# A graph network on one core: the gated messages in batches of 14, their gates in PSUM

## The chip, the core and the metric

The kernel runs on one core of one Trainium2 chip. The metric is the device time in microseconds of one execution. Three runs of the kernel before took 7233.45 us in the median (7215.12 to 7235.60).

## What is computed

Four blocks of a graph network over 6250 nodes and 200000 edges (96 features; edges sorted by their target `dst`): a graph convolution network with three layers, one with two, a message layer with gates, and attention over the edges. The change is in the third block:

```python
edge_input = jnp.concatenate([x[src], edge_attr], axis=-1)
messages = _gelu(edge_input @ mW1 + mb1) @ mW2 + mb2
gates = jax.nn.sigmoid(_gelu(edge_input @ gW1 + gb1) @ gW2 + gb2)
aggregated = jax.ops.segment_sum(messages * gates, dst, num_segments=x.shape[0])
```

`edge_attr` has 32 features. `mW2` is applied after the sum over edges, so what is summed for each node is gelu(message hidden) times gate, 96 wide, and the gate itself as a 97th column.

## The kernel before

Most of the span is the same in both kernels: lists and edge counts, five convolutions as dense products with a matrix of edge counts, and at the end dense attention. Between them lies the **sum pass** (`sum_pass` on each engine), which computes the gated sums. The products x @ mW1 and x @ gW1 with their biases have been stored to DRAM as rows of 192 numbers (`table_mg`).

The 200000 edges and some padding are 128 chunks (one in each partition) of 1568 steps. A batch is U = 16 steps, that is 16 edges in each of 128 partitions; there are 98 batches, two (h = 0 and 1) in each of ITER = 49 turns of a loop. All engines walk through the same batches and wait for each other by semaphores. For one batch:

- **SP** (SyncE) loads the 16 source indices of each partition (`si[h]`) and the edge attributes (`EA[:, h]`), one batch of the same h ahead, once the rows of batch (i, h) have landed; then it waits for the batch's sums and stores them to DRAM (`run_m`). These are all one queue, in order.
- **POOL** (GpSimd) issues 16 indirect DMAs (`gather`, L671), one for each step: each fetches 128 rows of `table_mg`, one into each partition of `G[:, h, j]`. Before a batch it waits until PE has used `G[:, h]` (`hidden_ready` of the batch two earlier) and until its indices have landed.
- **PE** (TensorE) multiplies the edge attributes by a block-diagonal weight (L933) into 8 banks of PSUM (`p_h`, two steps each), and, once the gathered rows have landed, adds them by a product with the identity (L939).
- **ACT** (ScalarE) applies gelu to each bank, into `A[:, h]` in SBUF (L1175).
- **DVE** (VectorE, `gated` and `sum_pass`) multiplies the gate half of `A` by the row of gate weights `gw2` (L1606), reduces it (L1609), waits for ACT's sigmoid in `small` (L1165), multiplies the message half by the gate (L1611), copies the gate as column 97 (L1613), and then makes a running sum over the steps, 16 dependent instructions (L1631). Where the target node changes the sum starts anew (`kp` is 0 there).

After the last batch 49 more gathers fetch, for each node, the running sum at its last edge. All 8 banks of PSUM belong to the hidden values in this stage: `p_e` (4), `p_tr` (2), `p_mm` (2).

`turns` (L381) runs a body once outside and then ITER - 1 times in a hardware loop; POOL's body has 32 gathers. The same U also sizes the batches of a second way (`scatter_pass`), which is taken only for inputs that the lists can't hold; it isn't executed here.

## Time and profile before

| | |
|---|---|
| median of three runs | 7233.45 us |
| profiled execution | 7202.21 us |
| its span | 7200.2 us |
| sum pass: first to last gather of edge rows | 2652.2 to 4967.1 us |
| POOL busy over the span | 3046.4 us (42%) |
| DVE busy over the span | 4317.5 us (60%) |
| PE busy over the span | 5293.9 us (74%) |
| hardware DMA queue / software (gathers) queue | 33.0% / 9.7% of 16 engines |

The shares are averages over stages with different limits. In the profile's map of the span in 40 slices (180 us each) the sum pass fills the slices 15 to 27. Times in the rows are from the span's start. A gather's row gives POOL's time to issue it, not the landing of its data.

### The profile page before, as it was taken

How to read it: one execution, taken by the hardware profiler on the slowest of the kernel's cores; microseconds unless marked ns; L12 is line 12 of the kernel's file. 1: busy time of each engine (PE TensorE's matmuls, PEld its weight loads, DVE VectorE, ACT ScalarE, POOL GpSimd, SP SyncE). 2: the span in 40 equal slices, each digit the busy share in tenths (PEclk: the TensorE clock that was granted, in tenths of full speed). 3: DMA queues.
4: the chain of work that ended last, by engine and by line, in shares of the span. 5: the costliest groups of instructions: out<-in, count | busy, mean ns of one | idle time of the engine just before them, and what ended most of it. 6: DMA issues, size and time to landing. Idle time of an engine off the chain costs nothing.

```text
span 7200.2 us, 99230 instructions
## 1 busy us (share of the span) xinstructions
PE 5293.9 (74%) x32240; PEld 2880.2 (40%) x32240; DVE 4317.5 (60%) x10357; ACT 2375.5 (33%) x3422; POOL 3046.4 (42%) x2919
## 2 busy tenths in 40 slices
PE   2787878999899976555555555554498888888888
PEld 2344444777677763223223222322332222222223
DVE  7999999332433445444444444444567777777776
ACT  1333333000100003223223222221156666666665
POOL 1000000000000016777777777776156666666665
PEclk8999999999899987777777777776699999999998
DMA  2111112768476856666666667665011111111110
GB/s 51 64 80 71 74 78 89 228 218 268 161 249 215 267 173 102 111 112 110 113 114 114 112 115 117 113 105 86 12 42 43 43 43 45 47 43 43 43 43 23
DMA packets 493720, 752.38 MB, mean 104 GB/s; under 512 B 294904, under 2 KB 397480, under 8 KB 487240
## 3 DMA queue, kind: packets, MB, share of 16 engines
q1 hardware_dynamic: 415336, 589.29, 33.0%
q0 software_dynamic: 78176, 160.32, 9.7%
q8 instruction: 131, 2.15, 0.1%
q14 instruction: 77, 0.63, 0.0%
HBM read 585.63 MB, written 163.82 MB: 104 GB/s over the span
## 4 chain that ended last, share of the span: by engine, by line
PE 29%; DVE 28%; POOL 16%; issue 15%; ACT 4%; DMA 3%; another core or an unknown queue 2%; DVEq 1%; SPq 1%; POOLq 0%; ACTq 0%
PE p_e L903 16%; POOL GA L671 12%; DVE VA L1784 9%; PE p_e L1021 5%; POOL VA L754 4%; ACT VA L1225 4%; DVE M L1402 4%; DVE VA L1402 4%; DVE VA L1400 2%; DVE M L1400 2%; PE p_mm L1010 2%; PE p_mm L868 2%; DMA GA<-table_mg,si 1%; PE p_tr L855 1%
## 5 line engine op out<-in xcount | busy, mean ns | idle before, releaser
L671 POOL DMA_INDIRECT GA<-table_mg,si x1568 | 1723.3, 1099 | 3187.2 <-DMA si<-in_src 2598.9
L1784 DVE TENSOR_TENSOR VA<-VA,p_mm 128x1024 f32<-128x1024 f32 (+1 forms) x1274 | 1420.6, 1156 | 482.6 <-POOL VA L754 454.0
L754 POOL TENSOR_SCALAR VA<-VA 128x1024 f32<-128x1024 f32 (+1 forms) x1274 | 1245.4, 996 | 814.1 <-ACT VA L1225 814.1
L1225 ACT ACTIVATE VA<-p_e 128x1024 f32<-128x1024 f32 (+1 forms) x1274 | 1174.4, 972 | 753.1 <-PE p_e L1021 752.9
L939 PE MATMUL p_e<-GA,C 128*128 128x384 f32 x784 | 428.1, 712 | 896.2 <-DMA GA<-table_mg,si 893.6
L1606 DVE TENSOR_TENSOR M<-GA,gw 128x1536 f32<-128x1536 f32 x98 | 172.5, 1760 | 1059.6 <-ACT GA L1175 684.8
L1035 PE MATMUL p_tr<-VA,GA 128*32 128x512 f32 (+1 forms) x5096 | 662.2, 593 | 0.5 <-DVE VA L1784 0.5
L939 PEld LDWEIGHTS p_e<-GA,C 128*128 128x128 f32 x784 | 212.2, 283 | 1100.2 <-DMA GA<-table_mg,si 945.5
L1021 PE MATMUL p_e<-T,GA 32*128 32x512 f32 x3528 | 632.8, 650 | 1.1 <-ACT VA L1225 0.8
L903 PE MATMUL p_e<-GA 128*128 128x288 bf16 x4802 | 609.6, 288 | 10.8 <-DVEq L1560 10.8
L903 PE MATMUL p_e<-GA,VA 128*128 128x288 bf16 x4802 | 608.3, 287 | 10.8 <-DVEq L1560 10.8
L1631 DVE SCALAR_TENSOR_TENSOR R<-R,kp,M 128x97 f32<-128x97 f32 x1568 | 507.1, 323 | 116.8 <-issue 0.3
L1175 ACT ACTIVATE GA<-p_e 128x384 f32<-128x384 f32 x392 | 188.5, 492 | 1176.1 <-PE p_e L939 605.3
L903 PEld LDWEIGHTS p_e<-GA 128*128 128x128 bf16 x4802 | 472.0, 98 | 132.5 <-DVEq L1560 11.2
L903 PEld LDWEIGHTS p_e<-GA,VA 128*128 128x128 bf16 x4802 | 471.5, 98 | 131.7 <-DVEq L1560 11.2
L1568 DVE TENSOR_REDUCE VA<-p_e 128x288 f32 (+1 forms) x196 | 89.7, 458 | 672.5 <-PE p_e L903 672.5
L1154 ACT ACTIVATE hT<-p_tr 96x512 f32<-96x512 f32 (+1 forms) x156 | 87.7, 565 | 1182.9 <-PE p_tr L855 1137.3
L836 PE MATMUL p_e<-VA 128*128 128x392 f16 x1176 | 284.4, 354 | 140.9 <-DVE VA L1402 113.7
L1402 DVE TENSOR_SCALAR VA<-EA 128x392 f16<-128x392 f16 x1176 | 372.2, 316 | 0.0
L1402 DVE TENSOR_SCALAR M<-EA 128x392 f16<-128x392 f16 x1176 | 372.0, 316 | 0.0
L933 PE MATMUL p_e<-BD,EA 128*128 128x384 f32 x784 | 291.6, 514 | 98.7 <-ACT GA L1175 77.9
L1130 ACT ACTIVATE GA<-p_e 128x392 bf16<-128x392 f32 x400 | 198.9, 497 | 341.1 <-PE p_e L836 341.1
(177 smaller groups left out, 6568.8 us busy)
## 6 DMA issues: line engine op xcount, KB each, us to landing
GA<-adj SPq DMA_DIRECT2D x98, 800.0 KB, 4.6
VA<-adj SPq DMA_DIRECT2D x98, 800.0 KB, 4.6
run_m<-R SPq DMA_DIRECT2D x98, 776.0 KB
GA<-adj SPq DMA_DIRECT2D x98, 768.0 KB, 4.4
VA<-adj SPq DMA_DIRECT2D x98, 768.0 KB, 4.4
H<-adj SPq DMA_DIRECT2D x56, 896.0 KB, 4.9
adj<-GA SPq DMA_DIRECT2D x25, 1568.0 KB, 5.1
adj<-VA SPq DMA_DIRECT2D x24, 1568.0 KB, 5.1
```

Of the source, the lines that this page charges most:

```text
L671: pool.indirect_dma_start(out=to, out_offset=None, in_=of, in_offset=bass.IndirectOffsetOnAxis(ap=at, axis=0)).then_inc(s, 16)
L754: pool.tensor_scalar(e, e, HIGH, LOW, ALU.min, ALU.max).then_inc(clipped, 1)
L903: mm = pe.matmul(p_e[b][:, 0:PARTS * D], blk[b][:, s * P:(s + 1) * P], parts[:, s, :, :].rearrange("p k f -> p (k f)"), start=s == 0, stop ...
L933: mm = pe.matmul(p_h[k][0:CH, 0:4 * D], EA[:, h, k // 2, :], BD[:, 2 * (k % 2):2 * (k % 2) + 2, :, :].rearrange("p a b f -> p (a b f)"), s ...
L939: pe.matmul(p_h[k][0:CH, 0:4 * D].rearrange("p (a f) -> p a f", a=2), C[0:CH, C_ID:C_ID + CH], G[0:CH, h, 2 * k:2 * k + 2, 0:2 * D], start ...
L1021: mm = pe.matmul(p_e[e][:, 0:across(b)], kT[rows, d * P:(d + 1) * P], qT[b][rows, 0:across(b)], start=True, stop=True, tile_position=(e * ...
L1035: mm = pe.matmul(p_tr[b % 2][e * HW:(e + 1) * HW, 0:across(b)], Vt[:, d, e, :], slot[k % SLOTS][:, e % 2, 0:across(b)], start=d == 0, stop ...
L1225: act.activation(slot[k % SLOTS][:, :, 0:across(b)], p_four[:, 2 * e:2 * e + 2, 0:across(b)], ACT.Exp).then_inc(exps_ready, 1)
L1400: dve.tensor_scalar(hot_lo[r], iota_lo, here[b][:, 3 * PER + k:3 * PER + k + 1], None, ALU.is_equal)
L1402: hot = dve.tensor_scalar(hot_key[r], iota_key, here[b][:, k:k + 1], None, ALU.is_equal)
L1631: op = dve.scalar_tensor_tensor(out=R[:, h, j, 0:MW], in0=before, scalar=kp[:, h, j:j + 1], in1=M[:, j, 0:MW], op0=ALU.mult, op1=ALU.add)
L1784: dve.tensor_tensor(e, e, p_mm[n % 2][:, 0:across(b)].unsqueeze(1).to_broadcast([P, 2, across(b)]), ALU.mult).then_inc(weighed, 1)
```

## The change

Batches have 14 steps instead of 16: 56 turns of two batches, 112 batches, and again 1568 steps. 14 steps fill 7 banks of PSUM. The eighth bank (`p_mm[1]`) holds a copy of the row of gate weights (`gate_row`, written once by DVE at the stage's start) and the gates (`gates`, written by ACT's sigmoid). L1606 and L1611 so read one operand from SBUF (`A`) and one from PSUM. The edge attributes of a batch still take 4 groups of 4 steps, the last with two steps of padding. POOL's gathers have a loop of their own: one turn outside, then 11 passes of a body with five turns (140 gathers). The buffers `GA` and `M` keep their size.

```diff
-U = 16
+U = 14
...
-BANKS = 8
-assert U == 2 * BANKS
+BANKS = 7
+TURN = 5
+assert U == 2 * BANKS and (ITER - 1) % TURN == 0
...
-        p_h = [*p_e, *p_tr, *p_mm]
+        p_h = [*p_e, *p_tr, p_mm[0]]
+        gate_row = p_mm[1][0:CH, 0:D]
+        gates = p_mm[1][0:CH, D:D + U]
...
-                turns(pool, body)
+                body(0)
+                with pool.Fori(0, (ITER - 1) // TURN) as i:
+                    for k in range(TURN):
+                        body(i * TURN + (k + 1))
...
-            def gate(i, h):
+            def gate(i, h, to):
                 act.wait_ge(logit_ready, i * 2 + (1 + h))
-                act.activation(small[:, 1, 0:U], small[:, 0, 0:U], ACT.Sigmoid, bias=sc[0:CH, 1:2]
-                               ).then_inc(gate_ready, 1)
+                act.activation(to, small[:, 0, 0:U], ACT.Sigmoid, bias=sc[0:CH, 1:2]).then_inc(gate_ready, 1)
...
-                        gate(i, h)
+                        gate(i, h, gates)
...
-            def gated(i, h, hid):
+            def gated(i, h, hid, row, gate):
 
                 dve.tensor_tensor(M[:, :, 0:D], hid[:, :, D:2 * D],
-                                  gw2[0:CH, :].unsqueeze(1).to_broadcast([CH, U, D]), ALU.mult)
+                                  row.unsqueeze(1).to_broadcast([CH, U, D]), ALU.mult)
                 dve.drain()
                 dve.tensor_reduce(small[:, 0, 0:U], M[:, :, 0:D], AX_X, ALU.add).then_inc(logit_ready, 1)
                 dve.wait_ge(gate_ready, i * 2 + (1 + h))
-                dve.tensor_tensor(M[:, :, 0:D], hid[:, :, 0:D],
-                                  small[:, 1, 0:U].unsqueeze(2).to_broadcast([CH, U, D]), ALU.mult)
-                return dve.tensor_copy(M[:, :, D:MW], small[:, 1, 0:U].unsqueeze(2))
+                dve.tensor_tensor(M[:, :, 0:D], hid[:, :, 0:D], gate.unsqueeze(2).to_broadcast([CH, U, D]), ALU.mult)
+                return dve.tensor_copy(M[:, :, D:MW], gate.unsqueeze(2))
 
             def sum_pass():
+
+                dve.tensor_copy(gate_row, gw2[0:CH, :])
+                dve.drain()
```

On DVE, at the start of the sum pass, the program before has (`GA` holds the gelu's output, `gw` is the row of gate weights, `small` holds logits and gates):

```order
L1619 COPY kp<-keep 128x16
L1606 TENSOR_TENSOR M<-GA,gw 128x16x96 [waits gelu_done]
L1609 TENSOR_REDUCE small<-M 128x16
L1611 TENSOR_TENSOR M<-GA,small 128x16x96 [waits gate_ready]
L1613 COPY M<-small 128x16
L1631 SCALAR_TENSOR_TENSOR R<-R,kp,M 128x97 x16
```

and now, at the same place (line numbers are those of the changed kernel):

```order
L1631 COPY p_mm<-gw 128x96
L1636 COPY kp<-keep 128x14
L1621 TENSOR_TENSOR M<-GA,p_mm 128x14x96 [waits gelu_done]
L1624 TENSOR_REDUCE small<-M 128x14
L1626 TENSOR_TENSOR M<-GA,p_mm 128x14x96 [waits gate_ready]
L1627 COPY M<-p_mm 128x14
L1648 SCALAR_TENSOR_TENSOR R<-R,kp,M 128x97 x14
```

The order is the same; both products have their second operand in PSUM, and each instruction is 14 steps wide.

On POOL, the loop of the gathers before:

```order
L385 UNCONDITIONAL_BRANCH
L385 ISA
L690 REGISTER_ALU [waits hidden_ready]
L671 DMA GA<-table_mg,si0 128x192 [waits idx_landed0]
L671 DMA GA<-table_mg,si0 128x192 x15
L671 DMA GA<-table_mg,si1 128x192 [waits hidden_ready,idx_landed1]
L671 DMA GA<-table_mg,si1 128x192 x15
L385 REGISTER_ALU
L385 COMPARE_AND_BRANCH
```

and the beginning of the loop now, with the first of its five turns and the head of the second:

```order
L705 UNCONDITIONAL_BRANCH
L705 ISA
L698 ISA [waits hidden_ready]
L679 DMA GA<-table_mg,si0 128x192 [waits idx_landed0]
L679 DMA GA<-table_mg,si0 128x192 x13
L679 DMA GA<-table_mg,si1 128x192 [waits hidden_ready,idx_landed1]
L679 DMA GA<-table_mg,si1 128x192 x13
L697 ISA
L698 ISA [waits hidden_ready]
```

The same waits stand ahead of each batch, after 14 gathers instead of 16, and the branch comes after 140 gathers instead of 32.

## Rows read from the trace of the kernel before

**Rows 1.** The page's map of the span in 40 slices, busy tenths of POOL.

```profile
POOL 1000000000000016777777777776156666666665
```

**Rows 2.** Engines by stretch: busy us of PE, PEld, DVE, ACT, POOL; PE clock, DMA share, GB/s.

```profile
2722.00:4968.00 2246.00, 1218.93 (x3087) 665.13 (x3085) 1035.03 (x2037) 647.17 (x1060) 1692.93 (x1536) 0.76 0.69 113
```

**Rows 3.** Groups by line and shape, 2700 to 5000: count, busy, mean ns; idle before.

```profile
L671 POOL DMA_INDIRECT GA<-table_mg,si x1536 | 1692.9, 1102 | 582.2 <-issue 526.5 <-remote 50.6 <-DMA si<-in_src 3.3
L1631 DVE SCALAR_TENSOR_TENSOR R<-R,kp,M 128x97 f32<-128x97 f32 x1568 | 507.1, 323 | 116.8 <-issue 0.3
L1606 DVE TENSOR_TENSOR M<-GA,gw 128x1536 f32<-128x1536 f32 x98 | 172.5, 1760 | 1059.6 <-ACT GA L1175 684.8 <-issue 373.7
L1611 DVE TENSOR_TENSOR M<-GA,small 128x1536 f32<-128x1536 f32 x98 | 172.4, 1759 | 36.7 <-ACT small L1165 32.6 <-issue 4.1
L1609 DVE TENSOR_REDUCE small<-M 128x16 f32<-128x1536 f32 x98 | 171.8, 1753 | 7.3
```

**Rows 4.** Timeline of POOL and DVE, one batch: start, duration, instruction, idle before.

```profile
3510.03 1.76 DVE L1606 TENSOR_TENSOR M<-GA,gw 128x1536 f32<-128x1536 f32 x1 [9.69 <-ACT GA L1175]
3510.38 2.23 POOL L671 DMA_INDIRECT GA<-table_mg,si  x1 [0.30 <-issue]
...
3512.92 0.94 POOL L671 DMA_INDIRECT GA<-table_mg,si  x1 [0.30 <-issue]
...
3513.99 1.76 DVE L1611 TENSOR_TENSOR M<-GA,small 128x1536 f32<-128x1536 f32 x1 [0.38 <-ACT small L1165]
3514.16 2.41 POOL L671 DMA_INDIRECT GA<-table_mg,si  x1 [0.30 <-issue]
...
3515.92 6.28 DVE L1631 SCALAR_TENSOR_TENSOR R<-R,kp,M 128x97 f32<-128x97 f32 x16
...
3518.15 0.94 POOL L671 DMA_INDIRECT GA<-table_mg,si  x1 [0.30 <-issue]
```

**Rows 5.** Timeline of DVE and POOL in the attention stage.

```profile
6003.40 4.77 DVE L1784 TENSOR_TENSOR VA<-VA,p_mm 128x1024 f32<-128x1024 f32 x4 [1.39 <-POOL VA L754]
6004.67 2.05 POOL L754 TENSOR_SCALAR VA<-VA 128x1024 f32<-128x1024 f32 x2 [0.37 <-ACT VA L1225]
```

**Rows 6.** Timeline around a long pause of POOL between two batches.

```profile
3451.88 4.81 PE L939 MATMUL p_e<-GA,C 128*128 128x384 f32 x8 [8.69 <-DMA GA<-table_mg,si]
...
3469.27 0.94 POOL L671 DMA_INDIRECT GA<-table_mg,si  x1 [0.30 <-issue]
...
3472.73 0.49 ACT L1175 ACTIVATE GA<-p_tr 128x384 f32<-128x384 f32 x1 [4.40 <-remote]
...
3475.16 0.94 POOL L671 DMA_INDIRECT GA<-table_mg,si  x1 [4.94 <-remote]
```

**Rows 7.** Timeline of POOL: one of the pauses that return every 112 gathers.

```profile
3502.86 0.94 POOL L671 DMA_INDIRECT GA<-table_mg,si  x1 [2.19 <-issue]
```

**Rows 8.** Who POOL waited for, 2700 to 4990: us, times, longest.

```profile
POOL GA L671 <- issue: 526.5, 1511, 30.9
POOL GA L671 <- remote: 50.6, 14, 5.3
POOL GA L671 <- DMA si<-in_src: 3.3, 5, 2.1
```

**Rows 9.** Timeline at the stage's beginning (third batch) and end.

```profile
2722.89 1.86 POOL L671 DMA_INDIRECT GA<-table_mg,si  x1 [30.91 <-issue]
...
4966.13 0.95 POOL L671 DMA_INDIRECT GA<-table_mg,si  x1 [0.30 <-issue]
...
5004.43 0.95 POOL L671 DMA_INDIRECT VA<-run_m,ends  x1 [37.35 <-DMA run_m<-R]
```

**Rows 10.** Timeline: a store of sums, a batch's last gather, and PE's start on it.

```profile
3522.44 0.41 SPq L512 DMA_DIRECT2D run_m<-R  x1
3523.16 0.95 POOL L671 DMA_INDIRECT GA<-table_mg,si  x1 [0.31 <-issue]
...
3533.44 4.98 PE L939 MATMUL p_e<-GA,C 128*128 128x384 f32 x8 [18.81 <-DMA GA<-table_mg,si]
```

More of the change, by code:

```diff
@@ L37 @@
 EG = 4
+UG = -(-U // EG)
 PIECES = 4
-BANKS = 8
-assert U == 2 * BANKS
+BANKS = 7
+TURN = 5
+assert U == 2 * BANKS and (ITER - 1) % TURN == 0
+ROOM = 16
 MW = D + 1
@@ L145, in build @@
         KV = VA[:, 0:TILES * 2 * D].rearrange("p (t f) -> p t f", t=TILES)
-        GA = sb("GA", [P, 2 * U * (GW + 2 * D)])
+        GA = sb("GA", [P, 2 * ROOM * (GW + 2 * D)])
         G = GA[:, 0:2 * U * GW].rearrange("p (h u f) -> p h u f", h=2, u=U)
-        A = GA[:, 2 * U * GW:].rearrange("p (h u f) -> p h u f", h=2, u=U)
+        A = GA[:, 2 * U * GW:2 * U * (GW + 2 * D)].rearrange("p (h u f) -> p h u f", h=2, u=U)
         R = sb("R", [CH, 2, U, AW])
-        M = sb("M", [CH, U, AW])
-        EA = sb("EA", [P, 2, EG, CH])
+        Mr = sb("M", [CH, ROOM, AW])
+        M = Mr[:, 0:U, :]
+        EA = sb("EA", [P, 2, UG, CH])
         keep = sb("keep", [CH, STEPS])
@@ L235, in build @@
         unit = (P + KEYS) // 2
-        m_flat = M[:, :, :].rearrange("p u f -> p (u f)")
+        m_flat = Mr[:, :, :].rearrange("p u f -> p (u f)")
         units = [m_flat[:, r * unit:(r + 1) * unit] for r in range(6)] + [
@@ L270, in build @@
         p_e = [p_four[:, k, :] for k in range(4)]
-        p_h = [*p_e, *p_tr, *p_mm]
+        p_h = [*p_e, *p_tr, p_mm[0]]
+        gate_row = p_mm[1][0:CH, 0:D]
+        gates = p_mm[1][0:CH, D:D + U]
+        pairs = [(g, c) for g in range(UG) for c in (0, 1) if EG * g + 2 * c < U]
+        assert len(pairs) == BANKS
         inputs_landed = sem("inputs_landed")
@@ L495, in load_edges @@
                     else:
[L496 removed]
+                        sp.wait_ge(edge_added, i * (2 * UG) + UG * (h - 1))
                 passed(sp, sp_passed)
[L498 removed]
+                sp.dma_start(EA[:, h, :, :], edge_t[:, bass.ds(i * (2 * UG) + UG * h, UG), :]
                              ).then_inc(edge_landed[h], 16)
@@ L911, in edge_products @@
                 pe.wait_ge(edge_landed[h], i * 16 + 16)
-                for g in range(U // EG):
-                    wait(pe, edge_added, i * (2 * U // EG) + (h * U // EG + g - 1))
+                for g in range(UG):
+                    wait(pe, edge_added, i * (2 * UG) + (h * UG + g - 1))
                     for c in (0, 1):
+                        if (g, c) not in pairs:
+                            continue
                         mm = pe.matmul(p_e[2 * (g % 2) + c][0:CH, 0:4 * D], EA[:, h, g, :],
@@ L1186, in body @@
                         if n == GATE:
-                            act.wait_ge(edge_added, i * (2 * U // EG) + (h + 1) * (U // EG))
+                            act.wait_ge(edge_added, i * (2 * UG) + (h + 1) * UG)
                             act.activation(gmg[h], gmg[h], ACT.Gelu).then_inc(gelu_done, 1)
-                            gate(i, h)
+                            gate(i, h, small[:, 1, 0:U])
                         if n == ATTEND:
@@ L1195, in body @@
                         wait_scattered(act, n, i, h)
-                        for k in range(U // 4):
-                            cp = act.activation(R[:, h, 4 * k:4 * k + 4, 0:width(n)],
-                                                p_c[k][0:CH, :].rearrange("p (u f) -> p u f", u=4)[:, :, 0:width(n)],
+                        for k in range(-(-U // 4)):
+                            n_u = min(4, U - 4 * k)
+                            cp = act.activation(R[:, h, 4 * k:4 * k + n_u, 0:width(n)],
+                                                p_c[k][0:CH, :].rearrange("p (u f) -> p u f", u=4)[:, 0:n_u, 0:width(n)],
                                                 ACT.Copy)
@@ L1593, in add_edges @@
             def add_edges(i, h):
-                for g in range(U // EG):
-                    dve.wait_ge(edge_product, i * (2 * U // EG) + (h * U // EG + g + 1))
+                for g in range(UG):
+                    dve.wait_ge(edge_product, i * (2 * UG) + (h * UG + g + 1))
                     for c in (0, 1):
+                        if (g, c) not in pairs:
+                            continue
                         rows = G[0:CH, h, EG * g + 2 * c:EG * g + 2 * c + 2, 0:2 * D]
@@ L1727, in body @@
                             dve.wait_ge(gelu_done, i * 2 + (1 + h))
-                            op = gated(i, h, gmg[h])
+                            op = gated(i, h, gmg[h], gw2[0:CH, :], small[:, 1, 0:U])
                         else:
@@ L1918 @@
         "row_heads": dst.reshape(-1, ROW)[:, 0], "src_rows": src.reshape(CH, STEPS).T, "dst_rows": dst.reshape(CH, STEPS).T,
-        "edge_t": edge_attr.reshape(CH, STEPS // EG, EG, ED).transpose(2, 3, 1, 0).reshape(P, STEPS // EG, CH),
+        "edge_t": np.pad(edge_attr.reshape(CH, 2 * ITER, U, ED), ((0, 0), (0, 0), (0, UG * EG - U), (0, 0))).reshape(
+            CH, 2 * ITER * UG, EG, ED).transpose(2, 3, 1, 0).reshape(P, 2 * ITER * UG, CH),
         "consts": shape_constants(),
```

8 lines of the change are left out of this document (3 added, 5 removed).

## The prediction

> **What bounds the kernel now.** I read the map of the span first [rows 1]: POOL works in the slices 15 to 27 and again in the attention; the change touches only the first of these, the sum pass. The table by stretch [rows 2] then gives from the third batch on 2246 us, in which POOL is busy 1693, DVE 1035, ACT 647 and PE 1219, the DMA engines 69%. The groups by line [rows 3] say what POOL's other 550 us are: nearly all idle time before a gather is "issue", spread over 1511 of them [rows 8], and the timeline shows it as 0.30 us ahead of each gather [rows 4]. So POOL issues gathers back to back, and the stage lasts as long as this: 98 x 16 = 1568 gathers in both kernels. All else waits for rows, and what makes POOL faster shortens the span one to one, as far as nothing else comes late.
>
> Its time from 2722.9 to 4967.1, 2244.2 us, for 1536 gathers, splits up so:
> - undisturbed gathers: 0.95 + 0.303 us each [rows 4], 1.253 x 1536 = 1924.6;
> - longer gathers: the mean is 1.102 instead of 0.95 [rows 3], 0.152 x 1536 = 233.5;
> - pauses: idle 582.2 [rows 3], less the 30.9 ahead of the third batch [rows 9], less 0.303 x 1536 = 465.4, leaves 86.
>
> **Longer gathers.** In the timeline of a batch a gather takes 2.23 us where it begins behind L1606, 2.41 behind L1611, and 0.94 under the reduction L1609 between the two and under the running sums L1631 behind them [rows 4]. That is up to 1.28 + 1.46 = 2.7 us for each of the 96 batches, 263 us, if every product hits one, and 233.5 were found. So it is these two products, both of whose inputs are in SBUF (`A` and `gw2` or `small`), that hold POOL up. L1631 also reads two tensors from SBUF, but is over in 0.32 us.
>
> With one input in PSUM, does the hold go? The nearest row is the attention's L1784, a product of an SBUF tile by PSUM with a broadcast, 128x1024: while four of them keep DVE busy for 4.77 us, POOL's two L754 run in 2.05 us, 1.02 each [rows 5]. POOL's instruction there reads and writes SBUF itself and isn't held. I take the gain as whole: 233.5 us. Its ends are 0 and 233.5; I see no reason for less than nothing.
>
> Ahead of this stands a rule that speaks against the change: the Trainium skill ("SBUF — State Buffer", section "Who interferes with whom") says that a two-input product with both inputs in SBUF contends only with GpSimd's reads, and infers that it doesn't delay the generation of DMA descriptors. By that, gathers wouldn't be held by the products, and the sum would lose its 233.5 us. The trace disagrees, 2.41 us behind L1611; an indirect gather has indices to read. The same section says that with at most one SBUF input the product doesn't contend at all, with which the attention's row agrees.
>
> **The rest on POOL.** The second part of the sum: the third batch waits until PE has used the first, at 2722.9 [rows 9]. By then 28 gathers are out instead of 32, so 1540 are left; PE has one bank less in each product ahead of it, some 1.3 us: start 2721.6. 1540 x 1.253 = 1929.6 us. Batches of 14 cost no gather more, and as each gather has the 0.30 us ahead of it within a batch and (apart from the pauses) between batches too, the number of batches costs POOL nothing.
>
> Pauses, 86 us: a timeline of all gathers shows 28 stretches over 0.5 us in the stage. Thirteen come every 112 gathers, one gather into a batch (2.19 us the typical one [rows 7], 33 us in all). They go by the count of gathers, not by a place in the loop, so they stay: 33. The others, 53 us, stand at the beginning of a batch: eleven of 3.6 to 5.3 us, mostly "remote" [rows 8], and four of 1 to 2 us right behind such a one, for indices. The instance: PE starts on batch 32 at 3451.9, but its banks reach ACT one by one in steps of 3 to 5 us until 3473.2, and POOL, done with batch 33 at 3470.2, goes on at 3475.2, 25 us after the last gather of batch 32 [rows 6]. All eleven have these 25 us (24 to 27). Why ACT gets them so slowly the trace doesn't say. POOL's cover is one batch of gathers, undisturbed 16 x 1.253 = 20.0 us. Now it is 14 x 1.253 = 17.5: the same event costs 7.5 us instead of 5, and eleven cost 82. Behind each the indices come late more often, since SP issues them behind the wait for the batch's sums: 14 us in all, by the four such waits before. I take 96 us in place of 53. The bounds are 0 (the events go) and, if one batch in five has one, 22 x 8.7 = 191.
>
> **The loop.** Both bodies end in one branch. Of the eleven long pauses three are at the loop's turn and eight at the middle of the body, and at most of the other turns the gap is 0.30 us as anywhere. So the branch costs nothing that the five-fold body could save. It adds no wait. Against it: if code of 140 gathers doesn't stay with the engine, each of 11 passes could pay a pause like the longest seen, 5 to 9 us: 0 to 100. I take 0.
>
> **What is beside the path.** A batch lasts 17.5 us now. DVE's chain in it: two products of 1.56, a reduction of 1.56, 0.4 for the sigmoid, 14 running sums of 0.39 (6.28/16 [rows 4]), 0.6 for copies and gaps, 11.1 us. Slower reads from PSUM are covered by the 6 us left; L1784 shows 4.77/4 = 1.19 us for 1024 columns [rows 5], against 1.76 for 1536, the same rate. ACT loads its tables 28 times more, 1.28 us each; its 11 us a batch fit too. PE's matmuls are as many as before. SP's queue has 14 more loads of attributes, each as large as before, and stores that are an eighth smaller: the 69% of 2246 us [rows 2] is 1550 us, which in 2060 us is 75%. What is queued behind: a store issued just ahead of a batch's last gather makes rows land 9 us after it instead of 1.7 (store at 3522.4, PE at 3533.4 [rows 10]). PE then is done at about +15, still inside 17.5, where the cover was 20 and more. The row of gate weights costs DVE 0.3 us once, ahead of the first gelu's end.
>
> **End of the stage.** Behind the last gather POOL waits 37.35 us for the last store [rows 9]. A bank less on PE and ACT, two steps less on DVE, and a smaller store: 3 us less.
>
> **Sum.** 2721.6 + 1929.6 + 33 + 96 = 4780.2, against 4967.1: -186.9, with the end -190 us. The profiled execution would take 7202.2 - 190 = 7012. The median of the runs is 31 us above the profiled one, and I carry that over: 7233.45 - 190 = 7043 us.
>
> **Rivals.**
> 1. *The pauses go.* The events with 25 us come from how batches of 16 fall against the stores, or the longer body ends them; then the stage ends at 4684 us, 283 less (286 with the end): 6947. For it: they come irregularly, and products no longer disturb POOL's pace. Against: nothing in the change touches PE's road to ACT.
> 2. *More pauses or a dear loop.* One batch in five has an event (95 us more), or the code is fetched on every pass (up to 100): 7090 to 7150. For it: at 17.5 us stores fall about 1.5 us behind a batch's last gather (gelu done at about +8, DVE's chain 11.1), just where PE and ACT work, and the 9 us of late landing leave hardly 2 us.
> 3. *The hold stays.* A product with PSUM holds POOL too, or the hold has another cause than the inputs: all of the 233.5 us stay, the pauses cost 96 - 53 = 43 more, and the later start and the end cancel: 7233 + 44 = 7277, or no change if pauses stay at 53. Against it: the attention's rows. (The Trainium skill's inference above, that such a product doesn't hold descriptors up, would lead here too.)
> 4. *Slower by late consumers.* One mechanism: with 17.5 us instead of 23 a batch the stores keep falling under PE's and ACT's work, so the slow hand-over from PE to ACT becomes the rule. At 8.7 us each, 33 events of 112 batches use up the 286 us; at one batch in two, 56, the stage loses 200 more than it gains: up to 7434. Eleven of 98 before speak against it.
>
> **Chances.** Forecast 0.52 (own range 7010 to 7080), rival 1 0.20, rival 2 0.19, rival 3 0.04, rival 4 0.05. A measurement tells 0.3% (22 us) from no change. Faster: the first three, 0.91. Same: half of rival 3 and a little of rival 4, 0.03. Slower: 0.06. The range 6940 to 7150 holds the first three and leaves the last two out.
>
> **What would show it.** In the trace after, gathers under both products at 0.95 us and a mean under 0.97 (right), or gathers of 2.2 us and more there (rival 3). A batch of POOL in 17.5 us, the stage from third batch to last gather in about 2059 us. Pauses over 0.5 us every 112 gathers as before, and pauses at batch beginnings of about 7.5 us, some ten of them; none is rival 1; 20 or more, or pauses at every tenth batch where the branch is, rival 2. DVE's products at 1.5 to 1.6 us. The forecast is wrong if DVE or ACT ends the idle time of POOL batch after batch.

## The result and the profile after: the time is the same, a little longer

The changed kernel takes 7253.28 us in the median of 20 runs (7236.77 to 7268.72), the kernel before in the same comparison 7227.93 (7205.84 to 7263.95): ratio 1.0036, interval 1.0024 to 1.0047. The forecast was 7043 us. The profiled execution has a span of 7265.2 us (before 7200.2).

The page's map of POOL in 40 slices shows the sum pass as wide as in [rows 1], with a 6 in each slice where a 7 was:

```profile
POOL 1000000000000016666666666665146666666665
```

The table by stretch answers to [rows 2] (busy us of PE, PEld, DVE, ACT, POOL; PE clock, DMA share, GB/s). POOL is busy 276 us less in the same stretch, and less gets done: 1498 gathers instead of 1536.

```profile
2722.00:4968.00 2246.00, 1298.88 (x2997) 684.70 (x2996) 1013.00 (x2033) 653.43 (x1069) 1416.54 (x1498) 0.74 0.68 112
```

The groups by line and shape, 2700 to 5050, answer to [rows 3]: count, busy, mean ns, idle before and what ended it.

```profile
L679 POOL DMA_INDIRECT GA<-table_mg,si x1540 | 1457.1, 946 | 879.8 <-issue 549.2 <-remote 178.4 <-DMA si<-in_src 115.5
L1648 DVE SCALAR_TENSOR_TENSOR R<-R,kp,M 128x97 f32<-128x97 f32 x1568 | 511.2, 326 | 130.6 <-issue 22.7
L1626 DVE TENSOR_TENSOR M<-GA,p_mm 128x1344 f32<-128x1344 f32 x112 | 174.1, 1554 | 38.4 <-ACT p_mm L1178 21.2 <-issue 17.1
L1621 DVE TENSOR_TENSOR M<-GA,p_mm 128x1344 f32<-128x1344 f32 x112 | 174.1, 1554 | 1083.9 <-ACT GA L1187 908.7 <-issue 175.1
L1624 DVE TENSOR_REDUCE small<-M 128x14 f32<-128x1344 f32 x112 | 174.0, 1553 | 8.2
```

The mean of a gather fell from 1102 to 946 ns. The timeline of POOL and DVE, as in [rows 4], shows no gather of 2.2 us any more, under neither product:

```profile
3478.85 1.55 DVE L1621 TENSOR_TENSOR M<-GA,p_mm 128x1344 f32<-128x1344 f32 x1 [17.68 <-ACT GA L1187]
3479.63 0.95 POOL L679 DMA_INDIRECT GA<-table_mg,si  x1 [0.30 <-issue]
...
3482.38 1.55 DVE L1626 TENSOR_TENSOR M<-GA,p_mm 128x1344 f32<-128x1344 f32 x1 [0.34 <-issue]
3483.38 0.95 POOL L679 DMA_INDIRECT GA<-table_mg,si  x1 [0.30 <-issue]
```

So POOL's gathers are 236 us shorter (1692.9 to 1457.1), and the gain is gone again. The stage from the third batch to the last gather takes 2304.1 us (2718.3 to 5022.3) instead of 2244.2. It is 1540 x (0.946 + 0.303) = 1923.5 us of gathers and 378.5 us of pauses over 0.5 us (each counted less the usual 0.30 us), where 83.2 were before. Of these, 73 pauses with 353.5 us stand at the beginning of a batch (before 15 with 50.5). Whom POOL waited for, 2700 to 5050 (us, times, longest; against [rows 8]):

```profile
POOL GA L679 <- issue: 549.2, 1473, 6.1
POOL GA L679 <- remote: 178.4, 32, 8.1
POOL GA L679 <- DMA si<-in_src: 115.5, 21, 7.8
```

The 21 pauses that end with the indices are part of the same lateness, as far as the rows tell: SP's queue is in order, and SP comes to them only behind the store of the sums before, which wait for PE, ACT and DVE. No run loads the indices earlier.

One such pause in the timeline, the counterpart of [rows 6]:

```profile
3558.11 5.49 PE L952 MATMUL p_e<-GA,C 128*128 128x384 f32 x8 [1.73 <-issue]
...
3564.90 0.81 PE L952 MATMUL p_mm<-GA,C 128*128 128x384 f32 x2
...
3566.88 1.40 SPq L520 DMA_DIRECT2D run_m<-R  x1
...
3573.00 0.95 POOL L679 DMA_INDIRECT GA<-table_mg,si  x1 [0.30 <-issue]
3573.18 0.01 SPq L496 DMA_DIRECT2D si<-in_src  x1
3581.02 1.64 ACT L1187 ACTIVATE GA<-p_e 128x384 f32<-128x384 f32 x4 [20.78 <-remote]
3581.18 0.33 SPq L506 DMA_DIRECT2D EA<-in_edge_t  x1
...
3582.06 0.94 POOL L679 DMA_INDIRECT GA<-table_mg,si  x1 [8.11 <-remote]
```

PE's records are over at 3565.7, but ACT gets the first bank at 3581.0 and then all at once; SP (waiting for PE to have used the attributes) and POOL go on at the same moment, 7 to 8 us after POOL's last gather was out. I measure this as the **delay**: from the start of PE's last product of a batch to the start of ACT's last gelu of it. It is 0.52 us at the least (where PE signals once a batch, in e5, e6 and e8, ACT does all gelus behind the signal, and it is 2.8 to 3.1 us at the least). Over 8 us it was in 12 of 96 batches before and in 44 of 110 after.

(A caution in reading: the ends of PE's records are modelled, as the profile's page says; the Trainium skill, "Perfetto Trace Analysis", section "Tensor Engine Instruction (MATMUL, LD_WEIGHTS)", adds that the signal goes out only when PSUM has acknowledged the write. In the pause shown ACT takes the four banks of `p_e` at 0.38 us from one to the next, 1.64 us for all four, while PE's own records for them fill 5.49 us. So the later of these banks, at least, were done before ACT heard of them; what held up the first signal the rows don't show.)

### The profile page after: what moved, and what is told of

It is laid out like the page before. It is cut to its first block, busy times and chain, and to the rows that moved or that the text cites. A ratio compares the mean times of both kernels' runs of the same rounds, so it can differ in the third digit from the quotient of the medians.

```text
span 7265.2 us, 99693 instructions
## 1 busy us (share of the span) xinstructions
PE 5417.3 (75%) x32240; PEld 2925.0 (40%) x32240; DVE 4331.3 (60%) x10428; ACT 2401.3 (33%) x3464; POOL 2804.6 (39%) x2919
## 4 chain that ended last, share of the span: by engine, by line
PE 31%; DVE 30%; issue 12%; POOL 10%; another core or an unknown queue 7%; ACT 5%; DMA 2%; DVEq 1%; SPq 1%; POOLq 0%; ACTq 0%
PE p_e L914 16%; DVE VA L1801 9%; POOL GA L679 5%; PE p_e L1034 5%; POOL VA L765 4%; ACT VA L1238 4%; DVE M L1415 4%; DVE VA L1415 4%; DVE VA L1413 2%; DVE M L1413 2%; PE p_e L952 2%; PE p_mm L1023 2%; PE p_mm L879 2%; DVE R L1648 2%
## 5 line engine op out<-in xcount | busy, mean ns | idle before, releaser
L679 POOL DMA_INDIRECT GA<-table_mg,si x1568 | 1483.5, 946 | 3482.5 <-DMA si<-in_src 2710.0
L952 PE MATMUL p_e<-GA,C 128*128 128x384 f32 x896 | 498.1, 723 | 528.4 <-DMA GA<-table_mg,si 483.3
L1621 DVE TENSOR_TENSOR M<-GA,p_mm 128x1344 f32<-128x1344 f32 x112 | 174.1, 1554 | 1083.9 <-ACT GA L1187 908.7
L1034 PE MATMUL p_e<-T,GA 32*128 32x512 f32 x3528 | 614.3, 651 | 1.1 <-ACT VA L1238 0.8
L946 PE MATMUL p_e<-BD,EA 128*128 128x384 f32 x896 | 374.5, 561 | 292.9 <-ACT GA L1187 191.4
L1187 ACT ACTIVATE GA<-p_e 128x384 f32<-128x384 f32 x448 | 210.9, 491 | 1075.3 <-PE p_e L952 435.6
L952 PEld LDWEIGHTS p_e<-GA,C 128*128 128x128 f32 x896 | 250.4, 290 | 766.8 <-DMA GA<-table_mg,si 535.5
L946 PEld LDWEIGHTS p_e<-BD,EA 128*128 128x128 f32 x896 | 186.5, 215 | 453.3 <-ACT GA L1187 221.5
```

Of the source, the lines that this page charges most:

```text
L679: pool.indirect_dma_start(out=to, out_offset=None, in_=of, in_offset=bass.IndirectOffsetOnAxis(ap=at, axis=0)).then_inc(s, 16)
L946: mm = pe.matmul(p_h[k][0:CH, 0:4 * D], EA[:, h, k // 2, :], BD[:, 2 * (k % 2):2 * (k % 2) + 2, :, :].rearrange("p a b f -> p (a b f)"), s ...
L952: pe.matmul(p_h[k][0:CH, 0:4 * D].rearrange("p (a f) -> p a f", a=2), C[0:CH, C_ID:C_ID + CH], G[0:CH, h, 2 * k:2 * k + 2, 0:2 * D], start ...
L1034: mm = pe.matmul(p_e[e][:, 0:across(b)], kT[rows, d * P:(d + 1) * P], qT[b][rows, 0:across(b)], start=True, stop=True, tile_position=(e * ...
```

## The experiments

Eighteen kernels ran in five groups (e1 to e4, e5 to e8, e9 to e12, e13 to e15, e16 to e18). The kernels of a group ran on one chip, together with runs of the kernel before, and each group had another chip. The letters of the theories are those of the expectation in which they stand; C is the five-fold body in the first group and the chip in the last. The columns: median of before on that chip and ratio to it; mean time of a gather's record; the stage from third batch to last gather, whole and per gather; pauses at batch beginnings, their number and sum; batches with a delay over 8 us (of 110, or 96 with 16 steps). All but the median and the ratio are worked out from each profile's timeline.

| kernel | before, ratio [interval] | gather | stage, per gather | pauses | delayed |
|---|---|---|---|---|---|
| before | | 1.102 | 2244, 1.461 | 15, 51 | 12 |
| after | 7228, 1.0036 [1.0024, 1.0047] | 0.946 | 2304, 1.496 | 73, 354 | 44 |
| e1 flat14 | 7227, 0.9986 [0.9972, 1.0000] | 0.948 | 2260, 1.468 | 76, 306 | 60 |
| e2 flat16 | 1.0041 [1.0028, 1.0055] | 1.102 | 2296, 1.495 | 24, 110 | 25 |
| e3 turns14 | 1.0039 [1.0024, 1.0054] | 0.946 | 2296, 1.491 | 76, 346 | 44 |
| e4 sbuf14 | 1.0027 [1.0012, 1.0042] | 1.066 | 2294, 1.490 | 51, 163 | 26 |
| e5 one14 | 7204, 1.0096 [1.0070, 1.0121] | 0.946 | 2328, 1.512 | 79, 378 | 61 |
| e6 one16 | 1.0015 [0.9998, 1.0032] | 1.094 | 2258, 1.470 | 29, 85 | 16 |
| e7 breaks14 | 1.0816 [1.0792, 1.0840] | 0.948 | 2858, 1.856 | 0 | 0 |
| e8 flat, one | 1.0012 [1.0002, 1.0023] | 0.951 | 2260, 1.468 | 93, 302 | 85 |
| e9 drain14 | 7228, 1.0313 [1.0281, 1.0345] | 0.950 | 2519, 1.636 | 0 | 0 |
| e10 tie14 | 0.9984 [0.9969, 0.9998] | 0.950 | 2271, 1.475 | 0 | 0 |
| e11 narrow14 | 1.0017 [1.0001, 1.0033] | 0.944 | 2292, 1.488 | 83, 344 | 48 |
| e12 drain16 | 1.0364 [1.0330, 1.0397] | 1.052 | 2546, 1.658 | 0 | 0 |
| e13 noedge14 | 7131, 0.9635 [0.9619, 0.9651] | 0.946 | 1951, 1.267 | 1, 1 | 0 |
| e14 double14 | 0.9646 [0.9630, 0.9662] | 0.946 | 1964, 1.276 | 5, 13 | 0 |
| e15 noedge16 | 1.0058 [1.0041, 1.0075] | 1.093 | 2226, 1.449 | 0 | 0 |
| e16 after again | 7203, 1.0063 [1.0038, 1.0088] | 0.946 | 2298, 1.492 | 76, 348 | 46 |
| e17 double14 again | 1.0137 [1.0111, 1.0163] | 0.946 | 2345, 1.523 | 87, 394 | 41 |
| e18 noedge14 again | 1.0008 [0.9995, 1.0022] | 0.950 | 2266, 1.471 | 56, 309 | 24 |

### Is it the store? e1_flat14, e2_flat16

Both store the sums from a buffer without gaps between the steps, so that a partition's 14 or 16 steps go out in one packet (5432 B in e1) instead of one of 388 B each.

```diff
+        RS = r_flat[:, 0:2 * U * MW].rearrange("p (h u f) -> p h u f", h=2, u=U)
...
-                        sp.dma_start(by_chunk(run_m)[:, at_batch(i, h), :], R[:, h, :, 0:MW]
+                        sp.dma_start(by_chunk(run_m)[:, at_batch(i, h), :], RS[:, h, :, :]
```

> The changed kernel, but the running sums of a batch lie without gaps in SBUF (97 columns a step instead of 97 of 100), so that the store of a batch is one stretch of 5432 bytes per partition instead of 1792 packets of 388 bytes. Theory A (the store's many small packets clog the way of PE's signals to ACT, SP and POOL): the pauses of POOL over 0.5 us fall from 380 us to under 100, the sum pass ends some 280 us earlier, the time is 6950 to 7030 us. Theory B (the pace of 17.5 us a batch is too fast for PE, ACT and DVE whatever the store looks like): within 1% of the changed kernel's 7253 us. Theory C (the five-fold loop body of the gathers makes the pauses): also unchanged.

> The kernel before, with the same gapless store (2048 packets of 388 bytes become 128 stretches of 6208 bytes). Theory A: the 86 us of pauses lose the 53 at the beginnings of batches, rows land 2 us behind a batch's last gather instead of 9 wherever a store goes just ahead; POOL stays bound with the products holding its gathers: 7228 - 50 = about 7175 us. Theory B: 7228 us, no change.

In e1 the DMA engines are busy 39% of the stretch instead of 68%:

```profile
2722.00:4968.00 2246.00, 1294.24 (x3064) 688.32 (x3062) 1034.39 (x2080) 653.62 (x1091) 1449.46 (x1529) 0.76 0.39 114
```

The delays don't go, they are in 60 batches instead of 44; the stage is 44 us shorter than in the changed kernel's profile, and with 16 steps 52 longer than in that of the kernel before. On their one chip e1 takes 7216 us beside 7250 of e3 below, which is the changed kernel but for a loop, and e2 7256 beside 7227 of the kernel before. So the form of the store has a say of some 30 us either way, theory A missed in both (it had 6950 to 7030 and 7175), and the store's many packets aren't what holds PE's signals up.

### The loop and the place of the gates: e3_turns14, e4_sbuf14

e3 is the changed kernel with POOL's loop of one turn a pass; e4 with the row of gate weights and the gates in SBUF.

```diff
# e3
-                body(0)
-                with pool.Fori(0, (ITER - 1) // TURN) as i:
-                    for k in range(TURN):
-                        body(i * TURN + (k + 1))
+                turns(pool, body)
# e4
-                        gate(i, h, gates)
+                        gate(i, h, small[:, 1, 0:U])
...
-                        gated(i, h, A[0:CH, h, :, :], gate_row, gates)
+                        gated(i, h, A[0:CH, h, :, :], gw2[0:CH, :], small[:, 1, 0:U])
```

> The changed kernel with the loop of the gathers as before: one turn of two batches in the body. Theory A and B: within 0.5% of the changed kernel (7253 us), pauses at batch beginnings as before. Theory C: pauses fall back to about 90 us, time about 6970 us.

> The changed kernel (batches of 14, five turns in the loop body), but gate weights and gates are read from SBUF again; the eighth bank is idle. The products then hold gathers by 2.7 us a batch again, 235 us in all. Theory A and B: the clogged hand-over between the engines needs the same time as in the changed kernel and the longer gathers cover part of it, so less than 235 us is added: 7300 to 7450 us. If the operands in PSUM themselves caused the pauses (theory D), pauses fall to about 90 us and the time is about 7200 us.

e3 is the changed kernel within the intervals: the five-fold body brings and costs nothing. In e4 the hold under the products is back:

```profile
L679 POOL DMA_INDIRECT GA<-table_mg,si x1540 | 1641.2, 1066 | 686.2 <-issue 527.2 <-remote 117.0 <-PE p_mm L952 37.9
```

1066 against 946 ns is 185 us more in gathers, and the pauses at batch beginnings are 191 us less; the stage stays at 2294. No theory had this: A and B had expected 7300 to 7450 us and D about 7200, and it is 7240, where e3 on the same chip has 7250. What the gathers lose, the pauses give back, and the other way round.

### Fewer signals: e5_one14, e6_one16, e8_flat_one14

PE signals once a batch, with its last bank; ACT and POOL wait for that (e8 also has the store of e1).

```diff
-                            act.wait_ge(hidden_ready, i * (2 * BANKS) + (BANKS * h + k + 1))
+                        act.wait_ge(hidden_ready, i * 2 + (h + 1))
```

> The changed kernel, but PE signals the hidden values once a batch, at the last bank, instead of after each of 7 banks; ACT waits once a batch. PE then sends 2 signals a batch (this and the one for the edge products) instead of 8. Theory E (while POOL issues gathers without a break, PE's signals leave only every 2 to 5 us and pile up, until POOL stops): with 2 signals in 17.5 us nothing piles up, the pauses at batch beginnings fall from 354 us to under 100, the sum pass ends 230 to 280 us earlier, the time is 6970 to 7030 us. Theory B (PE, ACT and DVE can't keep the pace of 17.5 us a batch): the gelus begin some 5 us later, so no gain, 7250 us or more.

> The kernel before with the same one signal a batch (2 instead of 9). Theory E: the 50 us of pauses at batch beginnings go, POOL stays bound by its gathers with the products holding some: 7228 - 50 = about 7180 us. Theory B: as before or a few us longer.

> The changed kernel with one signal a batch and with the gapless store of the running sums. Theory E: as the one with one signal, 6970 to 7020 us, a little faster as rows no longer land 9 us late behind a store. Theory B: 7215 us, as with the gapless store alone.

The one signal is late as well. Counted to ACT's first gelu, which is the signal alone, it comes over 8 us behind PE's last product in 51 of 110 batches of e5, 15 of 96 of e6 and 72 of 110 of e8. So it isn't the number of signals, and theory E missed in all three. The times are those of theory B (PE, ACT and DVE can't keep the pace); against B speak e10, e13 and e14 below, which have no delay over 8 us at 20.6, 17.7 and 17.9 us a batch.

### Breaks in POOL's issuing: e7_breaks14

```diff
# e7
                         for j in range(U):
                             gather(G[0:CH, h, j, 0:2 * D], table_mg, si[h][:, j:j + 1], rows_landed[h])
+                            if j in (4, 8):
+                                pool.drain()
+                                pool.memset(scratch[:, 3300:4500], 0.0)
+                                pool.drain()
```

> The changed kernel with two breaks in each batch of gathers: after the 5th and the 9th gather POOL clears 1200 columns that nobody reads, some 1.2 us each with the drains around it, as long as the products held it before. Theory E: PE's signals catch up in the breaks, the pauses at batch beginnings fall from 354 us to under 120, and the breaks themselves cost 112 x 2.6 = 290 us, so the time stays near 7200 us. Theory B: the slower pace of 20 us a batch covers the consumers too, same figures; but if the consumers are merely late by a fixed time, the pauses shrink one for one and the time is 7250 us. If the pauses stay at 350 us (neither), about 7500 us.

On the chip on which e5 and e8 had 61 and 85 delayed batches, e7 has none: the delay is at most 0.6 us in all 110. Timeline of one batch, with the first bank taken up 1.7 us after PE began:

```profile
3523.66 2.93 PE L956 MATMUL p_e<-GA,C 128*128 128x384 f32 x4 [16.27 <-DMA GA<-table_mg,si]
...
3525.10 1.10 POOL L704 MEMSET VA<- 128x1200 f32 x1 [3.62 <-issue]
...
3525.35 0.49 ACT L1191 ACTIVATE GA<-p_e 128x384 f32<-128x384 f32 x1 [17.05 <-PE p_e L956]
```

So PE's signals can be in time on this chip. The run alone doesn't say whether the breaks do it or the slower pace of 26 us a batch that they bring; e10 below does. And a break is dear: the drain behind four gathers takes 1.94 us in the mean, the one behind ten 3.39 (2.14 to 6.98); with the memsets and the second drains this makes the stage 553 us longer, where 290 had been expected.

### One drain, or one earlier wait: e9_drain14, e12_drain16, e10_tie14

e9 and e12 have a bare drain behind the seventh (eighth) gather. e10 has no drain, but a wait at that place until PE has signalled the whole batch before:

```diff
# e10
+                            if j == 6 and not (h == 0 and first(i)):
+                                pool.wait_ge(hidden_ready, i * (2 * BANKS) + (BANKS * h))
+                                passed(pool, pool_passed)
```

> The changed kernel with one bare drain of POOL in each batch, behind the seventh gather (the run with two breaks of drain, memset, drain a batch had PE's last bank reach ACT 0.52 us behind PE in all 110 batches, against over 8 us in 44 batches of the changed kernel; but its breaks cost 3.4 us each and its pace was 25.5 us a batch, so it doesn't tell a break from a slower pace). Theory E (PE's signals are held up while POOL issues gathers without a break): one break a batch lets them through; a bare drain should cost 1.6 to 2 us, about 200 in all, and the pauses at batch beginnings, 353 us, fall under 60: the stage from third batch to last gather about 2150 to 2220 us instead of 2304, ratio 0.98 to 0.99. Theory F (whatever POOL does, gathers get through no faster than about 1.46 us each, and what is gained at one place comes back as a pause): the pauses fall by what the drains cost, the stage stays at 2280 to 2310 us, ratio 0.997 to 1.002.

> The kernel before with one bare drain of POOL in each batch, behind the eighth of 16 gathers. Theory E: the delays over 8 us between PE and ACT (12 of 96 batches) go and with them 45 us of pauses at batch beginnings, while 98 drains cost 1.6 to 2 us each, 160 to 195 us: stage 2350 to 2400 us against 2244, ratio 1.015 to 1.022. Theory F: at 1.46 us a gather the drains come out of nothing but the pauses, 2244 + 160 to 195 less 50 at most, much the same; this run tells the price of a drain and whether the delays go with breaks at a pace of 25 us.

> The changed kernel with one more wait of POOL in each batch: ahead of the seventh gather it waits until PE has signalled all banks of the batch before. When the signals are in time it costs nothing (PE is done about 6.3 us behind a batch's last gather, the wait stands 7.5 us behind it). Theory E: when they are late POOL stops early in the batch, and the signals come within some us of the stop, as they came in a burst after the stops at batch beginnings: stops of 2 to 4 us at the wait in the batches concerned, hardly any pause left at batch beginnings, delays over 8 us between PE and ACT in under 10 batches; stage 2150 to 2300 us. Theory F: stops of together 300 us or more, stage 2280 to 2310 us, ratio 0.997 to 1.003.

Whom POOL waited for in e9, 2710 to 5210, and in e10, 2700 to 5000:

```profile
POOL GA L679 <- issue: 1048.5, 1522, 10.0
```

```profile
POOL GA L679 <- issue: 466.8, 1446, 2.3
POOL GA L679 <- remote: 186.1, 52, 4.3
POOL GA L679 <- PE p_mm L955: 183.3, 50, 26.1
```

My price for a bare drain, 1.6 to 2 us, was wrong, and with it both theories' figures for the stage of e9 (it is 2519 us) and of e12 (2546). POOL's idle time at the drain is 5.6 us in the mean in e9 (3.0 to 10.0; less the usual 0.30 us, 588 us in all) and 5.1 in e12 (3.0 to 9.4). What sets its length is in the traces: the landing of the gathers already issued. Here are two drains of e9, the first with no store of sums near, the second right behind one:

```profile
3501.89 0.95 POOL L679 DMA_INDIRECT GA<-table_mg,si  x1 [0.30 <-issue]
...
3505.88 0.95 POOL L679 DMA_INDIRECT GA<-table_mg,si  x1 [3.05 <-issue]
...
3521.49 0.70 SPq L520 DMA_DIRECT2D run_m<-R  x1
3522.17 0.95 POOL L679 DMA_INDIRECT GA<-table_mg,si  x1 [0.30 <-issue]
...
3532.37 0.95 POOL L679 DMA_INDIRECT GA<-table_mg,si  x1 [9.25 <-issue]
```

If the DMA packets of the trace are counted off in order, 48 for each gather, the gap is 2.1 us in the mean longer than the last gather takes to land behind its record, and the two go together in e9's 110 drains with a correlation of 0.99. Where packets of a store start within 1 us of that record's end (52 drains) the gap is 7.9 us in the mean, elsewhere 3.6. The same holds in e7: the drain behind ten gathers takes 5.3 us beside a store and 2.4 without one, and the drain behind four, 1.9 us, never stands beside a store. So a drain is dear above all where a store is under way with it; the number of gathers ahead of it has a smaller part (2.4 against 1.9 us in e7).

In e10 no batch is delayed by over 3.8 us and no pause is left at a batch's beginning, at the pace of the changed kernel (20.6 and 20.9 us a batch). So it is POOL's stops that let the signals through, not a slower pace; both theories had said this much. And little is won: POOL stops at the seventh gather in 100 batches, 3.14 us in the mean, 314 us in all, and the stage takes 2271 us. Theory F had stops of 300 us and more, but the stage is 9 us under its range; theory E's wide range (2150 to 2300) holds it. The place of the stops can be chosen; their sum stayed above 300 us.

### Half the bytes: e11_narrow14

Each gather fetches 96 numbers a row; PE reads them twice. The result leaves out the true gate half.

```diff
-                            gather(G[0:CH, h, j, 0:2 * D], table_mg, si[h][:, j:j + 1], rows_landed[h])
+                            gather(G[0:CH, h, j, 0:D], table_mg.rearrange("n (a f) -> (n a) f", a=2), si[h][:, j:j + 1],
+                                   rows_landed[h])
```

> The changed kernel with gathers of 96 instead of 192 numbers a row: half the bytes, as many gathers and as many rows; PE reads the one half twice, so that its work stays. The result leaves out the true gate half. Theory E (the issuing on POOL holds the signals up): nothing changes, pauses at batch beginnings 300 to 380 us, stage 2260 to 2310 us, ratio 0.995 to 1.003. Rival T (the traffic of the gathers holds them up, or bounds the rate): the pauses fall under 150 us, stage under 2130 us, ratio under 0.985.

Stage 2292 us, 344 us of pauses, as theory E had it: it isn't the bytes of the gathers. Nor does their data pile up: a gather's last packets start 2.8 us in the mean and at most 8.2 us behind its record in the changed kernel, and 1.5 and at most 2.9 in e8, which has the most delays.

### PE's work, and a surprise: e13_noedge14, e14_double14, e15_noedge16

```diff
# e13, e15: the edge product for the last bank only (its result leaves the others' edge attributes out)
+                            if k == BANKS - 1:
                                 mm = pe.matmul(p_h[k][0:CH, 0:4 * D], EA[:, h, k // 2, :],
# e14: each edge product twice
+                            for done in (True, False):
                                 mm = pe.matmul(p_h[k][0:CH, 0:4 * D], EA[:, h, k // 2, :],
...
-                                           start=True, stop=False)
+                                               start=True, stop=done)
```

> The changed kernel with the product of the edge attributes done for the last of its seven banks only (the result leaves out the edge attributes of the others): PE has 8 products a batch instead of 14, all loads and signals stay. Theory H (PE is the bound beside POOL: 14 products of 0.64 us at the higher clock and 1.28 us at the lower are 9.0 to 17.9 us a batch, and what its records show as done is not done yet): PE's last bank reaches ACT within 1 us in nearly all batches, the pauses at batch beginnings fall from 353 to under 60 us, the stage from 2304 to 2010 to 2100 us, ratio 0.965 to 0.98. Theory E (the signals are held up by POOL's issuing, whatever PE does): pauses stay at 300 to 380 us, stage 2260 to 2310 us, ratio 0.997 to 1.004.

> The changed kernel with each product of the edge attributes made twice, the second in place of the first: PE has 21 products a batch instead of 14. Theory H: the seven more products cost 4.5 us a batch at the higher clock and 9 us at the lower, and come out in full where PE is the bound: stage 2304 + 490 to 990, about 2800 us or more, ratio over 1.06. Theory E: they lie in the idle time of PE (11 of 21 us a batch are busy): stage 2290 to 2350 us, ratio 1.002 to 1.01.

> The kernel before with the product of the edge attributes done for the last of its eight banks only. Theory H: the 50 us of pauses at batch beginnings go and POOL's gathers with their holds are the bound alone: stage 2185 to 2210 us instead of 2244, ratio 0.993 to 0.996; with e13 the two show the 130 to 190 us that the change would bring if nothing else were late. Theory E: stage 2230 to 2260 us, ratio 0.998 to 1.002.

Eight products of PE a batch instead of 14 brought 3.7%, a little more than theory H had; but 21 products brought 3.5% too, where H had expected over 6% more time. Both can't come from PE's work. E missed as well. The kernel with 16 steps and less work for PE (e15) is 0.6% slower than the kernel before, which neither theory had. And the kernel before itself was at 7131 us on this chip, 71 to 97 us under its medians on the others. That raised the last question.

### The same on another chip: e16_after_again, e17_double14_again, e18_noedge14_again

The changed kernel unedited, and e14 and e13 once more.

> The changed kernel itself, unedited, beside the two variants of PE's work and the kernel before, all on one chip. Theory C (it depends on the chip or its state whether PE's signals are held up): where the kernel before takes about 7130 us, this one takes 6850 to 6900, stage 1950 to 2000 us, no pauses at batch beginnings, ratio 0.96 to 0.97; where the kernel before takes 7200 to 7230, it takes 7230 to 7270 as the first time. Theory H (PE's work decides): 7230 to 7270 us wherever it runs, ratio 1.003 to 1.02, while the doubled and the halved products bring 3.5%.

> The changed kernel with each product of the edge attributes made twice, once more. Theory C: the same as the unedited changed kernel beside it, within 0.5%: pauses of 300 us and more where that has them, none where that has none. Theory H: 3.5% under the kernel before again, whatever the unedited one shows.

> The changed kernel with the product of the edge attributes done for the last bank only, once more (the result leaves out the edge attributes of the others). Theory C: within 0.5% of the unedited changed kernel beside it. Theory H: 3.6% under the kernel before again.

The same program ran on the chip of the fourth group (e14) and on that of the fifth (e17). The map of POOL, e14 and then e17:

```profile
POOL 1000000000000004777777777774166666666665
```

```profile
POOL 1000000000000016666666666665246666666665
```

The stretch 2722 to 4600 (columns as above), e14 and then e17:

```profile
2722.00:4600.00 1878.00, 1572.49 (x4419) 889.41 (x4419) 999.76 (x1996) 661.75 (x1054) 1391.63 (x1472) 0.92 0.77 131
```

```profile
2722.00:4600.00 1878.00, 1368.49 (x3710) 758.30 (x3708) 834.89 (x1672) 526.31 (x881) 1165.62 (x1232) 0.87 0.63 110
```

The gathers of the sum pass by line, e14 and then e17:

```profile
L679 POOL DMA_INDIRECT GA<-table_mg,si x1538 | 1455.3, 946 | 506.8 <-issue 490.6 <-PE p_mm L953 9.7 <-DMA si<-in_src 6.4
```

```profile
L679 POOL DMA_INDIRECT GA<-table_mg,si x1540 | 1457.1, 946 | 925.4 <-issue 518.2 <-DMA si<-in_src 223.3 <-remote 146.5
```

A gather's record is 946 ns on both. On the one POOL's idle time is 507 us, nearly all of it the 0.30 us ahead of each gather; on the other 925. The stage takes 1964 and 2345 us, delayed are 0 and 41 batches. The changed kernel itself has the ratio 1.0063 on this second chip, the two variants beside it 1.0137 and 1.0008. So it is the chip, or a condition that it was in, that decides whether the stage is held to about 1.46 to 1.52 us a gather; theory H is out. PE's work has a small say: with the fewer products (e18) it takes 0.5% less than the unedited kernel and has 24 delayed batches instead of 46, with the doubled ones (e17) 0.7 to 0.8% more, which is beyond theory C's 0.5%.

## Why the prediction was wrong, step by step

- **Longer gathers, 233.5 us: right.** 1102 ns fell to 946, 1066 with the operands back in SBUF (e4). The timeline shows 0.95 us under both products. Rival 3 is out. Out as well, for this kernel, by the 2.23 and 2.41 us under products of two SBUF tensors, is what the Trainium skill infers ("SBUF — State Buffer", "Who interferes with whom"), that a product of two SBUF tensors doesn't delay the generation of descriptors.
- **The rest on POOL: right, nearly.** The stage begins at 2718.3 instead of the forecast 2721.6; 1540 gathers at 1.249 us are 1923.5 us, forecast 1929.6.
- **Pauses: the failed step.** I took "the same event costs 7.5 us instead of 5, and eleven cost 82", with 14 more for indices and 33 for the periodic ones, together 129 us, and as the upper end 191 at batch beginnings. The pauses over 0.5 us came to 378.5 us, those at batch beginnings 353.5. The size of one was no worse than I had it (4.8 us in the mean); their number was, 73 instead of some fifteen, and I had carried the number over without knowing its cause. What the runs show in its place is a floor: on all chips but one the stage needs 1.46 to 1.52 us a gather in all 14 profiles of kernels without breaks or drains, whether POOL's own share is 1.25 or 1.41 us. Before, the two were so close (1.405 of gathers and their gaps, 0.056 of pauses) that the pauses looked like accidents. The error begins ahead of that step, where I wrote that what makes POOL faster shortens the span one to one, "as far as nothing else comes late": it did come late, and more often the faster POOL was.
- **The loop, 0: right** (e3 against the changed kernel, 1.0039 and 1.0036).
- **What is beside the path.** DVE's products take 1.554 us, forecast 1.56, and the running sums 0.326 each. DVE's and ACT's own work wasn't what came late; PE's signals were.
- **End of the stage: not right.** Behind the last gather the span is 2242.9 us long, before 2233.1, forecast 3 less. In e16 it is 2220.9, so single profiles differ there by more than the term.
- **Rivals.** Rival 4 (0.05) is the one that came: the slow hand-over from PE to ACT in 44 batches, where it put its break-even at 33. Its reason, that the stores fall under PE's work, has little for it: with the store in one packet a partition the delays stayed (e1, e8). Its size, up to 200 us more, was too large, since the pauses only take back what gathers gain, and 60 us beyond. Rival 2's sign, 20 pauses or more at batch beginnings, was there too, but it had put their price at 95 us. Rival 1 (the pauses go) is what the chip of e13 to e15 shows: by its end of the stage at 4684 us the stage takes 1962 us, and e13 and e14 take 1951 and 1964.

What the change is worth on that chip can be read from e13 and e15, the same cut of PE's work in either kernel: spans 6863.7 and 7157.9, 294 us less, of which the stage is 274.5. Of this the gathers are 220 (0.147 x 1536, less 5 us for the four gathers that e13 has more). The other 54 are the thirteen pauses that return every 112 gathers (25.8 us in e13, 79.6 in e15): in e15 they take 6.4 us in the mean and twelve of them, of 4.4 to 8.5 us, stand beside a store of sums (over 900 of its packets within 2 us), in e13 2.2 and none does. That the sum is near rival 1's 286 is thus in part luck, for rival 1 left these pauses alone. Against the kernel before itself, which has no profile there, e13 and e14 are 263 and 255 us faster in the median. The unedited changed kernel wasn't run on that chip; e14 does all that it does and seven products a batch more.

**Open.** What holds PE's signals back while POOL issues without a stop, and why one chip of the five doesn't show it. That POOL's stops let the signals through is shown (e10 at the changed kernel's pace, e7, e9 and e12 at slower ones). That one and the same cause sets the floor and delays the signals is argued; it isn't data of the gathers that piles up (above). No profile of the kernel before and no drain was taken on the chip of e13 to e15, and whether it was the chip or a passing condition of it can't be told from one group of runs. The chip of the first profiles of the two kernels isn't known.

## What to carry to other kernels

An engine that issues back to back isn't proven to be the bound by its own records: take its rate down and up on purpose (here e4: 185 us more in the gathers, the same stage) before a gain on it is counted one to one. Rare pauses that have one length and end together on several engines may be the first signs of a limit close by, and then their number is no constant: don't carry it over before their cause is known. A drain behind DMA issues has no fixed price: look when the data already asked for lands. And where a gain hangs on such a limit, measure it on more than one chip: here the same program (e14, e17) was 3.5% faster than the kernel before on one and 1.4% slower on another.

## What the runs showed of the hardware

- A product of DVE with one operand in PSUM doesn't hold an indirect gather of GpSimd up (0.95 us); with both in SBUF it does (up to 2.41 us; mean of all gathers 1.066 us in e4 against 0.946).
- A drain of GpSimd behind indirect gathers ended with the landing of the last one, though that gather's record had ended after 0.95 us: in e9 the next gather began 1.7 to 3.9 us behind the landing, after gaps of 3.0 to 10.0 us, 3.6 in the mean without a store near and 7.9 beside one.
- With GpSimd issuing gathers without a break, PE's signal reached ACT up to 18.1 us after the start of the last of PE's records (e6, counted to ACT's first gelu), on four of the five chips of the experiments.
- More work for PE raised its granted clock (2722 to 4600 us; 0.5 and 1.0 stand for 1.2 and 2.4 GHz) from 0.75 in e16 to 0.87 in e17, and from 0.69 in e13 to 0.92 in e14 on the other chip. It didn't shorten the stage: 2298 and 2345 us on the one, 1951 and 1964 on the other.
